# Three normalisations on ScalarE and three block sums in another order, ahead of the first product of a two-layer graph and feed-forward network

## What is computed

```python
x = x + L0_gnn(layernorm(x))      # attention over 20000 edges, 4 heads
x = x + L0_ffn(layernorm(x))      # "rails"
x = x + L1_gnn(layernorm(x))      # graph convolution
x = x + L1_ffn(layernorm(x))      # shared expert and 8 routed ones
```

```python
xr = x.reshape(b, t, RAILS, RAIL_W)                    # 64 rails of 16
y = jnp.einsum('btri,hrij->bthrj', xr, rail_maker)
z = jnp.einsum('bthrj,hrkj->bthrk', y, rail_up_proj)   # 4 heads, 64 wide
h = jax.nn.gelu(z.reshape(b, t, -1), approximate=False)
out = h @ w_cproj.T                                    # 1024 x 16384
```

## Time and profile before

| | us |
|---|---|
| runs of the kernel before | 2591.76, 2594.21, 2595.81 |
| their median | 2594.21 |
| the profiled execution, span from its first to its last instruction | 2589.7 |
| the profiled execution's own time outside the span | not listed apart |
| TensorE busy | 2465.5 (95% of the span) |
| VectorE busy | 1968.1 (76%) |
| ScalarE busy | 1230.4 (48%) |
| mean granted TensorE clock | 0.978 of full speed |

### The profile page before, as it was taken

How to read it: one execution, slowest core, us unless ns; L and a number is a source line. 1 busy time by engine, 2 the same in 40 slices (tenths; PEclk the granted TensorE clock), 3 DMA queues, 4 the chain that set the end, 5 groups by cost and what they waited for, 6 DMA issues and landing times. The chain is left out here.

```text
span 2589.7 us, 34729 instructions
## 1 busy us (share of the span) xinstructions
PE 2465.5 (95%) x12652; PEld 1666.1 (64%) x12652; DVE 1968.1 (76%) x2504; ACT 1230.4 (48%) x1413; POOL 143.8 (6%) x173
## 2 busy tenths in 40 slices
PE   6999299889999999999999999999999989999998
PEld 4666287756666666666666666666666556568776
DVE  7876799798888897797797788788788756665422
ACT  6322676565555455445545545545544235522111
POOL 1000000010000000000000000000000011000222
PEclk9999699989999999999999999999999999999999
DMA  5211311143232232322421422422331045836993
GB/s 164 63 39 39 67 40 40 67 141 62 73 63 57 75 61 57 88 49 55 95 57 41 96 56 41 96 56 47 88 105 49 1 136 178 264 135 211 353 379 109
DMA packets 145389, 252.12 MB, mean 97 GB/s; under 512 B 67128, under 2 KB 82106, under 8 KB 138838
## 3 DMA queue, kind: packets, MB, share of 16 engines
q1 hardware_dynamic: 135378, 231.40, 31.3%
q0 software_dynamic: 4928, 10.25, 1.6%
q10 hardware_dynamic: 4932, 8.30, 0.9%
HBM read 204.01 MB, written 49.33 MB: 98 GB/s over the span
## 5 line engine op out<-in xcount | busy, mean ns | idle before, releaser
L1761 PE MATMUL wide_ps<-keep_own_room,rails_hid_hi 128*125 128x512 f16 x4200 | 1250.7, 379 | 5.2 <-DVE rails_hid_lo L1478 3.2
L1761 PE MATMUL wide_ps<-keep_own_room,rails_hid_lo 128*125 128x512 f16 x2100 | 796.4, 379 | 0.0
L1761 PEld LDWEIGHTS wide_ps<-keep_own_room,rails_hid_hi 128*125 128x125 f16 x4200 | 564.7, 137 | 312.5 <-issue 6.4
L1761 PEld LDWEIGHTS wide_ps<-keep_own_room,rails_hid_lo 128*125 128x125 f16 x2100 | 286.9, 137 | 167.0 <-issue 0.6
L1253 ACT ACTIVATE rails_hid_hi<-rails_raw_a,keep_scale_hidden 128x1000 f16<-128x1000 f32 x210 | 274.5, 1334 | 209.5 <-DVE rails_raw_a L1497 90.8
L1478 DVE SCALAR_TENSOR_TENSOR rails_hid_lo<-rails_raw_a,keep_scale_hidden,rails_hid_hi 128x1000 f16<-128x1000 f32 x210 | 312.1, 1516 | 41.7 <-ACT rails_hid_hi L1253 41.6
L1243 ACT ACTIVATE rails_raw_a<-wide_ps,keep_scale_gelu 128x1000 f32<-128x1000 f32 (+1 forms) x192 | 181.6, 951 | 323.6 <-PE wide_ps L1746 320.2
L1532 DVE SCALAR_TENSOR_TENSOR keep_X<-wide_ps,rails_out_scale,keep_X 125x1024 f32<-125x1024 f32 x180 | 198.6, 1103 | 132.3 <-PE wide_ps L1761 132.3
L1486 DVE SCALAR_TENSOR_TENSOR keep_own_room<-carried_w_land,rails_w_scale,keep_own_room 128x2048 f16<-128x2048 f32 x105 | 246.0, 2343 | 0.7 <-ACT keep_own_room L1268 0.7
L1268 ACT ACTIVATE keep_own_room<-carried_w_land,rails_w_scale 128x2048 f16<-128x2048 f32 x105 | 208.9, 1990 | 9.8 <-DVE carried_w_land L1516 5.7
L1228 ACT ACTIVATE rails_raw_a<-carried_w_land 128x2048 f32<-128x2048 f32 x64 | 121.7, 1902 | 141.9 <-DMA carried_w_land<-cproj 141.7
(11 more groups left out here) (476 smaller groups left out, 3359.3 us busy)
## 6 DMA issues: line engine op xcount, KB each, us to landing
carried_w_land<-cproj SPq DMA_DIRECT2D x79, 1024.0 KB
ffn_w_up<-split_d SPq DMA_DIRECT2D x9, 2048.0 KB
keep_own_room<-W SPq DMA_DIRECT2D x11, 1024.0 KB, 5.8
ffn_w<-W SPq DMA_DIRECT2D x11, 1024.0 KB
rails_xs<-xt_d SPq DMA_DIRECT2D x124, 78.1 KB
keep_comb_hi<-W SPq DMA_DIRECT2D x8, 1024.0 KB, 7.2
split_d<-graph_high SPq DMA_DIRECT2D x16, 512.0 KB, 6.6
keep_X<-split_d SPq DMA_DIRECT2D x4, 2048.0 KB
```

Source lines behind the costliest of these rows:

```text
L1761: mm = nc.tensor.matmul(ps[0:P, t, :], hid[(q + b) % 2][l][:, k, t * P:(t + 1) * P], w[(q + b) % 2][r][:, k, :], start=(k == 0 and i == 0) ...
```

## The change

Three things are moved or rewritten; the arithmetic done is the same but for rounding.

- **Normalisation.** Tiles 4, 6 and 8 are normalised on ScalarE, as `Identity(X * rstd_up + shift)`, where `shift = -mean * rstd_up` is a new 125 x 10 table that VectorE makes in two 125x5 instructions (`shift_of`). VectorE keeps tiles 2, 3, 5, 7 and 9. TensorE's `turn` waits for a semaphore of its own for those three tiles. VectorE's order around them changes too: `late_stats` stands ahead of `x_lo(1)`, `late_layer_of` ahead of `x_lo(2)`, `late_rstd_of` and `normalise(5)` ahead of `x_lo(3)`.
- **Sums of the W blocks.** `b11` is summed first, behind `x_hi(2)`; `b12` behind `x_hi(6)`; `b22` behind both high parts of the first hidden block. Before they stood behind `x_hi(5)`, `x_hi(3)` and `x_hi(7)`.
- **VectorE behind the first product's low parts.** `t3`, which changes `b22` in place and so needs its sum, moves behind both pieces of `a_lo` and behind the difference of the quarters of `X`.

```diff
@@ gpsimd
-                for name in ("b12", "b11", "b22"):
-                    spread_top(name, 0)
+                def first_top(name, n):
+                    pool.wait_ge(summed, n)
+                    nc.gpsimd.partition_all_reduce(tops[:, TOP[name]:TOP[name] + 1], sums[:, TOP[name]:TOP[name] + 1], 128,
+                                                   bass.bass_isa.ReduceOp.max).then_inc(top_set, 1)
+
+                for n, name in enumerate(("b11", "b12", "b22")):
+                    first_top(name, n + 1)
@@ scalar
+                def normalise(t):
+                    act.wait_ge(xt_turned, t - 2)
+                    act.wait_ge(shift_set, 1 if t < HALF_T else 2)
+                    nc.scalar.activation(xn[t % 3], X[:, t, :], ACT.Identity, bias=shift[:, t:t + 1],
+                                         scale=rstd_up[:, t:t + 1]).then_inc(xn_act_set, 1)
+
                 for t in range(TILES - 1):
                     x_hi(t)
-                    if t == 4:
+                    if t == 1:
+                        act.wait_ge(taken, HALF_T)
+                    if t == 2:
+                        w_sum("b11", 0, "a12", None)
+                    if t == 3:
                         act.wait_ge(late_layer, 1)
...
-                    if t == 3:
+                    if t + 3 in NORM_ACT:
+                        normalise(t + 3)
+                    if t == 6:
                         w_sum("b12", 0, "a12", None)
-                    if t == 5:
-                        w_sum("b11", 0, "a12", None)
-                    if t == 7:
-                        w_sum("b22", 0, "a12", None)
...
                 a_hi(0, 0, 0, 1)
+                w_sum("b22", 0, "a12", None)
                 w_hi(0, 1, 0)
@@ vector
+                def shift_of(lo, hi):
+                    nc.vector.scalar_tensor_tensor(shift[:, lo:hi], mean_var[:, lo:hi, 0], -1.0, rstd_up[:, lo:hi], ALU.mult,
+                                                   ALU.mult).then_inc(shift_set, 1)
+
...
                 attention_out()
+                shift_of(0, HALF_T)
                 normalise(2)
                 x_lo(0)
                 normalise(3)
+                late_stats()
                 x_lo(1)
-                late_stats()
-                normalise(4)
+                late_layer_of()
                 x_lo(2)
-                late_layer_of()
-                x_lo(3)
                 late_rstd_of()
                 normalise(5)
-                normalise(6)
+                shift_of(HALF_T, TILES)
+                x_lo(3)
                 x_lo(4)
                 normalise(7)
                 x_lo(5)
-                normalise(8)
                 x_lo(6)
...
                 a_lo(0, 0, 0, 0)
+                a_lo(0, 0, 0, 1)
+                dve.wait_ge(xn_set, 5)
+                dve.wait_ge(xn_act_set, len(NORM_ACT))
+                nc.vector.tensor_tensor(quarter_of(0, 1), quarter_of(0, 1), quarter_of(1, 1), ALU.subtract)
                 t3(0)
-                a_lo(0, 0, 0, 1)
                 scale_of(1, 0)
-                dve.wait_ge(xn_set, TILES - 2)
-                nc.vector.tensor_tensor(quarter_of(0, 1), quarter_of(0, 1), quarter_of(1, 1), ALU.subtract)
                 w_lo(0, 1, 0)
@@ tensor
                 def turn(t):
-                    if t >= 2:
-                        pe.wait_ge(xn_set, t - 1)
+                    if t in NORM_ACT:
+                        pe.wait_ge(xn_act_set, NORM_ACT.index(t) + 1)
+                    elif t >= 2:
+                        pe.wait_ge(xn_set, t - 1 - sum(a < t for a in NORM_ACT))
```

More of the change, by code:

```diff
@@ L1040, in rails @@
         late_layer, late_std, late_rstd = c.sem("late_layer"), c.sem("late_std"), c.sem("late_rstd")
+        NORM_ACT = (4, 6, 8)
+        shift, shift_set, xn_act_set = c.sb("shift", [P, TILES], F32), c.sem("shift_set"), c.sem("xn_act_set")
         xn_set, xt_turned, xt_hi_set, xt_lo_set = [c.sem(n) for n in ("xn_set", "xt_turned", "xt_hi_set", "xt_lo_set")]
@@ L1224, in w_sum @@
                     k = TOP[name]
-                    if not isinstance(u, int) or 4 * u + k >= 1:
+                    if not isinstance(u, int) or u >= 1 or name == "b21":
                         act.wait_ge(summed, 4 * u + k)
+                    elif name != "b11":
+                        act.wait_ge(summed, 1 if name == "b12" else 2)
                     junk = raw[spent][:].rearrange("p h f -> p (h f)")[:, 0:K4 * BANK].rearrange("p (k d) -> p k d", k=K4)
@@ L1417, in scale_of @@
                 def scale_of(k, u):
-                    dve.wait_ge(top_set, 4 * u + k + 2)
+                    dve.wait_ge(top_set, 1 if k == 0 and isinstance(u, int) and u == 0 else 4 * u + k + 2)
                     if k == 0:
```

## The result

The changed kernel takes 2598.97 us (median of 13 runs, 2595.70 to 2601.73), the kernel before 2594.21 us (13 runs, 2591.76 to 2596.97). The ratio is 1.0018, with a 95% interval of 1.0010 to 1.0025: slower by 2.6 to 6.5 us, 4.8 by the medians. The forecast was 2598.5 us, +4.3.

What follows compares the result with a forecast made beforehand. Transfers were taken to bound the start of product 0, then the gelus of `a21`. Added 2.81 + 2.28 us less 0.78 gave +4.3, so 2594.2 + 4.3 = 2598.5 us; range 2592.5 to 2602.0 us.

Steps and rivals of the forecast that it cites:

- The bound: Ahead of product 0, transfers bind and VectorE has slack; in product 0, delaying `a21`'s gelus delays TensorE one for one.
- The normalisation: One normalisation on ScalarE at 1024 columns takes 1.14 us, with bounds of 0.80 and 2.00 us.
- The start of product 0: The first matmul of product 0 moves by 0 to +0.6 us, taken as 0.
- rival B: Higher clock at the hidden matmuls and tile 9 starts product 0 1.5 us sooner: +2.8, 2597.0 us; chance 0.12.
- The chain on VectorE: Between products: low piece, difference, `t3`, `scale_of(1)` run in sequence, delaying `w_hi` of product 1 and `a21`'s gelus: +4.3 us.
- TensorE's wait: TensorE stands still for 4.3 us before part 2 of `a21`, which runs at 548.6 us.
- The clock: After the 4.3 us pause TensorE's clock drops, losing 1.65 us in product 0, swallowed by the later 1.84 us pause.
- Rival A: In product 0 the clock's drop outlasts its cover, losing 3.3 us: +5.8, or 2600.0 us; chance 0.20.
- The sum: Whole kernel: +4.3 us, +3.8 to +5.2 with the bounds; span 2594.0, median 2598.5 us.
- GpSimd: Clearing of `acc` behind the reduction of `b22` runs 540.6 to 547.1 us, hidden since VectorE asks at about 553.

Runs made afterwards that it cites:

- front_again: The kernel of front_only (changed front, VectorE's old order) run once more; one run, stage 1464.9 us, against 1464.7 in the kernel before.
- order_only: Kernel before, with only VectorE's order changed: `t3` and the quarters' difference between the last low piece and `scale_of(1)`; 2597.77 us, ratio 1.0014.
- late_only: Kernel before with its own front, but `b22` summed behind the first hidden block's high parts and VectorE's new order behind it; 2597.30 us, ratio 1.0012.
- gelu_first: Changed kernel with the three gelus of `a21` ahead of `w_hi` of product 1 on ScalarE; 2600.20 us, ratio 1.0026 to the kernel before.
- before_gelu: Kernel before with the gelus of parts 0 and 1 of `a22` ahead of the high parts of product 1's hidden block; 2594.11 us against 2594.13.
- before_take: before_gelu with the addition of node tiles 0 and 1 ahead of the low pieces on VectorE, run twice; 2592.66 and 2592.07 us against 2594.43.
- q_last: Changed kernel with the difference of the quarters moved back behind `scale_of(1)`; 2595.00 us, ratio 1.0007 to the kernel before.
- t3_early_gelu: Changed front with `b22` summed behind tile 4, `t3` and `scale_of(1)` in the prologue, gelus as in before_gelu; 2594.05 us, ratio 1.0000 to the kernel before.
- front_only: Changed kernel's front, but `b12` summed behind tile 4's high part, `b22` behind tile 6's, and VectorE's old order; 2594.86 us, ratio 1.0003 to before.

## Why the prediction was right

- **The bound.** Right: the advance of the normalisations died in the wait for the store, and the load of the first half went out at 526.71 both times. front_again, with the front alone, lies 0.2 us from before. Over all profiles the new front's load went out later rather than sooner (21.93 us behind the first high part on average, 21.58 with the old).
- **The normalisation.** 1.14 us was taken, 1.24 measured, well inside the bounds. The Trainium skill (ScalarE: Activation LUTs, What ACT_TABLE_LOAD costs) gives 280 ns and 0.833 ns for each element when one operand is read per partition, and about 93 ns for a second; an estimate from these figures is 1.23 us for 1024 elements, and the trace agrees. `w_hi` of product 0 came at 529.03 where 529.4 was reckoned.
- **The start of product 0.** Taken as 0, measured -0.63. The mechanism was rival B's, at less than half its size (1.5 us), and four of the seven executions with the new front had no sign of it. So it belongs to this execution and can't be counted as an effect of the change.
- **The chain on VectorE.** Right by each term, +4.16 us where +4.3 was summed: low piece 1.78 (1.77), difference 2.82 (2.81), `t3` 2.29 (2.28), `w_hi` at 8.53 us behind the first product's start (before 4.37) where 8.6 was reckoned. order_only shows that it is the whole cost, late_only that the front has no part in it.
- **TensorE's wait.** 4.3 was said, 3.81 measured. TensorE came to the place only at 544.0, 7.8 us behind its start instead of 7.4, held up before parts 0 and 1 of `a21` by their transfer: the weight load there waited 0.78 us for it, 0.18 before.
- **The clock.** Right in the main: after the wait, 0.80 from 548.6 to 555.0, and the pause before part 2 of `a22` shrank from 1.84 to 0.65 us. TensorE was ready for that part 5.75 us later than before (counted from the first product, its wait left out), where it had begun part 2 of `a21` 4.14 later: 1.6 us went to the clock, close to the 1.65 reckoned. The pause took up 1.2 of them. The other 0.4 got through by a way that the prediction did not look at: part 2 of `a21` itself ran at the low level, 1.01 us instead of 0.59, and the third gelu waited 0.54 us for it. `s3` waited for that gelu (to 549.96, while `w_lo` was done at 549.16), and the high parts of product 1 and the gelus of `a22` come behind `s3`. It began 13.75 us behind the first product instead of 9.19, 4.56 later, with `w_hi` only 4.16 later. Rival A was close: in late_only and order_only no pause was left at all. Part 2 of `a22` came 20.28 and 20.56 us behind the first product's start there and 20.26 in the changed kernel, so in order_only another 0.3 got through.
- **The sum.** +4.3 us forecast; +4.3 at the last product, +4.8 by the medians. That the profile meets the forecast to 0.1 us is partly luck: two terms put at nothing had opposite signs, 0.63 gained at the start and 0.4 lost through the clock. Part 2 of `a22` was 3.93 later; without the early start it would have been 4.56, and the last product 4.9 later, nearer to late_only and order_only (stage +5.2 and +5.0). The reckoned span of 2594.0 us was 1.6 too low, and what lies around the span was put at 4.5 us where this execution has 2.0: two errors that cancel in part in the absolute number, and neither touches the difference.
- **GpSimd.** The clearing of `acc` was put at 540.6 to 547.1 and ran from 541.91 to 548.48; it stayed covered, as VectorE asked for it only behind `s3`, which began at 549.99.

## What to carry to other kernels

When an instruction is moved behind a later sum, look at what it leaves behind: `t3` had run partly in some 1.3 us in which VectorE would have waited anyway, and in its new place all of it was on the path, together with work that had been beside it. Follow the chain to the slowest taker in each engine's fixed order, here `w_hi` with three gelus behind it, and do it for every chain through the place: curing one of two equally long ones (gelu_first) gains almost nothing and can cost clock. An advance ahead of a wait for a transfer was worth nothing here, though it took three operations off VectorE, and the last wait of a stretch is worth removing only together with the next one (before_gelu against before_take).

## What the runs showed of the hardware that was not expected

A reduction over partitions on GpSimd took 2.78 us instead of the usual 0.36 when it began 0.25 us after the start of VectorE's float32 difference of 2.82 us, and ended (542.05) just after that one did (541.84). late_only (2.67 us) and gelu_first (2.78 us) show the same, and so do later reductions beside a VectorE float32 difference of 2.75 us (128x2500): 0.66 us in the kernel before, 1.03 in q_last, 2.82 in t3_early_gelu, the longer the more of the difference was still to run. Each ended 0.21 or 0.22 us behind VectorE's instruction. In q_last, where the first such reduction began 0.05 us ahead of `t3`, it took 0.35. It cost nothing here, as `scale_of(1)` came later anyway.

The clock of TensorE in the prologue differs from execution to execution of one kernel. front_only had 0.50 for all of its window from 537 to 545 us, front_again 0.79 over 536.8 to 545, and part 2 of `a22` moved by 1.5 us with it, 0.4 of them through the later start of product 0. That is a third of the effect studied here.
